# Flamingo block: mLSTM heads weighted in pairs, vector work regrouped around them, the second LoRA weight prepared one stage earlier, one unread matrix product per batch

## The reference, cut to what matters

```python
x = x + tanh(g_xattn[0]) * _L0_xattn_ref(_layernorm(x), ctx, ctx, ...)   # mLSTM
x = x + tanh(g_ffn[0]) * _L0_ffn_ref(_layernorm(x), ...)                 # LoRA FFN
x = x + tanh(g_xattn[1]) * _L1_xattn_ref(_layernorm(x), ctx, ...)        # attention
x = x + tanh(g_ffn[1]) * _L1_ffn_ref(_layernorm(x), ...)                 # mixture of experts
# in the mLSTM, per sequence:
log_f = log_sigmoid(fg); cs = cumsum(log_f)
log_D = where(tril, cs[:, None] - cs[None, :], -inf) + ig
D_mat = exp(log_D - max(log_D))
C = (q @ k.T / sqrt(32)) * D_mat
normalizer = maximum(abs(C.sum(-1)), exp(-max(log_D)))
h = (C / (normalizer + 1e-6)) @ v            # then a layer norm over all heads, times ln_scale
# in the FFN, per weight:
wq = clip(round(w / scale), -128, 127) * scale   # scale = max|w| / 127
h = x @ wq.T + b + 2 * (x @ A.T) @ B.T           # the kernel adds 2 * B @ A to wq once
```

## Time and profile before

| | |
|---|---|
| median of three runs | 1334.13 us |
| the profiled execution | 1336.97 us, span of its instructions 1335.4 us |
| PE busy, over the span | 1203.9 us, 90% |
| DVE, ACT, POOL busy | 872.2, 710.9, 430.8 us |
| mean granted TensorE clock | 0.939 of 2.4 GHz |
| heads stage, first weighing to last update of x | 83.9 to 243.8 us |

### The profile page before, as it was taken

The page is one execution under the profiler, slowest core; times in us unless marked ns, Lnnn a source line. Parts: engine busy times, 40 slices in busy tenths (PEclk is TensorE's granted clock), DMA queues, the critical chain, the costliest instruction groups (busy, mean ns, idle before and its releaser), DMA issues. The chain is left out here.

```text
span 1335.4 us, 28816 instructions
## 1 busy us (share of the span) xinstructions
PE 1203.9 (90%) x9632; PEld 1009.7 (76%) x9633; DVE 872.2 (65%) x2027; ACT 710.9 (53%) x1582; POOL 430.8 (32%) x559
## 2 busy tenths in 40 slices
PE   7868989799999579999999986889989999997998
PEld 3335666698989456666666655879989999997998
DVE  4748778445454457777877755666757677765676
ACT  2357667446354136666666663325655555554553
POOL 1137766523130200111101001476422323221773
PEclk9968888899999869999999997889989999999999
DMA  9144542100000623343433403567745555543773
GB/s 298 54 147 175 179 154 96 48 0 0 0 0 1 113 57 90 82 113 74 97 96 76 97 3 118 204 226 262 228 130 165 172 163 161 179 158 108 269 226 117
DMA packets 97631, 164.71 MB, mean 123 GB/s; under 512 B 12264, under 2 KB 71836, under 8 KB 95228
## 3 DMA queue, kind: packets, MB, share of 16 engines
q1 hardware_dynamic: 87643, 136.11, 33.1%
q0 software_dynamic: 9264, 27.01, 6.4%
q10 hardware_dynamic: 624, 0.32, 0.1%
HBM read 103.66 MB, written 33.69 MB: 103 GB/s over the span
## 5 line engine op out<-in xcount | busy, mean ns | idle before, releaser
L1390 DVE TENSOR_REDUCE c_mx<-c_s 128x2 f32<-128x512 f32 x256 | 164.3, 684 | 74.7 <-PE c_s L1532 74.6
L1313 ACT ACTIVATE c_probs<-c_t 128x512 f32<-128x512 f32 x256 | 139.0, 595 | 8.5 <-PE c_t L1554 5.7
L2346 ACT ACTIVATE de_g_full<-de_hid,d_e_bias 128x256 f32<-128x256 f32 x156 | 77.5, 497 | 105.2 <-PE de_hid L34 105.2
L32 PE MATMUL de_hid<-de_zt_hi,d_e_hi 128*128 128x256 f32 x312 | 90.6, 290 | 1.4 <-DVE de_zt_lo L2370 1.4
L942 ACT ACTIVATE b_g_full<-b_hid,b_b 128x512 f32<-128x512 f32 x64 | 44.3, 692 | 86.8 <-PE b_hid L34 70.4
L1532 PE MATMUL c_s<-c_kt,c_qt 48*128 48x256 f32 x512 | 65.0, 333 | 26.9 <-DVE c_mx L1390 26.9
L34 PE MATMUL de_y_ps<-d_w_hi,de_g_lo 128*128 x312 | 88.2, 283 | 0.0
L32 PE MATMUL de_y_ps<-d_w_hi,de_g_hi 128*128 x312 | 88.1, 282 | 0.0
L33 PE MATMUL de_y_ps<-d_w_lo,de_g_hi 128*128 x312 | 88.0, 282 | 0.0
L1251 POOL CAST c_ct_hi<-c_c_raw 128x512 fp32r<-128x512 f32 x15 | 9.2, 611 | 243.1 <-PE c_misc L34 243.1
L34 PE MATMUL de_hid<-de_zt_hi,d_e_lo 128*128 128x256 f32 x312 | 87.2, 279 | 0.0
(11 more groups left out here) (377 smaller groups left out, 4132.8 us busy)
## 6 DMA issues: line engine op xcount, KB each, us to landing
d_e_raw<-in_w SPq DMA_DIRECT2D x39, 514.0 KB, 3.8
a_mb<-a_maxima SPq DMA_DIRECT2D x16, 1024.0 KB, 4.8
d_z_in<-d_z_rows POOLq DMA_DIRECT2D x39, 256.0 KB, 3.9
d_y_rows<-de_ys SPq DMA_DIRECT2D x39, 256.0 KB, 2.2
c_kt<-c_k_hi SPq DMA_DIRECT2D x64, 128.0 KB, 3.1
c_qt<-c_q_hi SPq DMA_DIRECT2D x64, 128.0 KB, 3.3
d_zt_kept<-d_w_hi SPq DMA_DIRECT2D x32, 256.0 KB, 2.5
d_w_hi<-d_zt_kept SPq DMA_DIRECT2D x16, 512.0 KB, 4.3
```

The source lines that it names most:

```text
L32: tensor.matmul(out, lhs_hi, rhs_hi, start=start, stop=False)
L1313: act.activation(probs[h % PR][:], t_ps[k][:], ACT.Exp).then_inc(exp_done, 1)
L1390: dve.tensor_reduce(mx[n % 2][:, :, k, p:p + 1], s_ps[h % SB][:], AX.X, ALU.max).then_inc(max_done, 1)
L2346: act.activation(g_full[:, m, :], hid[m][:, 0:TOK], ACT.Gelu, bias=bias[u][:, m:m + 1]).then_inc(gelu_full, 1)
```

## The change

Five things are done.

1. `weigh` handles two heads in one instruction (`PAIR = 2`): `a_decay`, `a_c_mat` and `a_qk` become one tensor each, and the instruction reads two banks.
2. On DVE `h_stat` moves behind head 3 and `h_norm` behind head 7. The statistics and the norm for the FFN are taken one tile per batch (batches 6 to 9 and 11 to 14) instead of four at once. The w2 steps leave the stage.
3. The w2 steps move to the end of `mlstm_gates`: quantising and adding on DVE, the high part in two pieces on ACT between `turn(7)` and `gates(7)`, the low part on DVE.
4. `a_mb` gets three buffers, so that its load is issued and POOL's `masks` run one batch earlier. On ACT `keep_outputs` for groups 0 and 1 stands behind `decays` of head 3, group 2 behind head 6 and group 3 behind head 7.
5. PE gets one 128x256 product of the identity with `a_ln_s` per batch (1 to 14) ahead of `scores(n, 1)`. It is written to `a_hp` and read by nobody.

```diff
@@ mlstm_gates, scalar
+            def split_w2(half):
+                act.wait_ge(summed_w2, 1)
...
             for n in range(STEPS):
                 turn(n)
+                if n == STEPS - 1:
+                    split_w2(0)
+                    split_w2(1)
                 gates(n)
@@ mlstm_gates, vector
                 if i == STEPS:
+                    quantise(1)
+                    add_delta_w2()
                     low_part()
+                    low_part_w2()
@@ mlstm_heads
-    W2_AT, HI_AT, LO_AT = 2, 7, 8
-    STATS_AT, RSTD_AT, Z_AT = 9, 10, 11
+    STATS_AT, RSTD_AT, Z_AT = 6, 10, 11
+    MR = 3
+    PAIR = 2
+    FILL = 1
@@ sync
-                after(sync, decay_done, 2 * (n - 1) * H)
-                sync.dma_start(mb[u][:], m_dram[n].partition_broadcast(P)).then_inc(m_loaded[u], 16)
+                after(sync, decay_done, 2 * (n + 1 - MR) * H)
+                sync.dma_start(mb[n % MR][:], m_dram[n].partition_broadcast(P)).then_inc(m_loaded[n % MR], 16)
@@ gpsimd
             values(0)
+            masks(1)
             pool.wait_ge(ready, 1)
             for n in range(B + 2):
                 if n >= 2:
                     h_rstds(n - 2)
+                if n + 2 < B:
+                    masks(n + 2)
                 if n + 1 < B:
-                    masks(n + 1)
                     values(n + 1)
@@ scalar
                     decays(n, h)
-                    if n > 0 and h in (0, 2, 3):
-                        keep_outputs(n - 1, max(h, 1))
-                    if h == H - 1:
-                        keep_outputs(n, 0)
+                    if n > 0 and h == H // 2 - 1:
+                        keep_outputs(n - 1, 0)
+                        keep_outputs(n - 1, 1)
+                    if n > 0 and h == H - 2:
+                        keep_outputs(n - 1, 2)
+                    if n > 0 and h == H - 1:
+                        keep_outputs(n - 1, 3)
@@ vector, weigh
-                dve.wait_ge(qk_done, k + 1)
-                dve.wait_ge(decay_done, 2 * k + 2)
-                after(dve, cv_done, k + 1 - CR)
-                dve.scalar_tensor_tensor(out=c_mat[h % CR][:], in0=qk[h % QUAD][:, 0:W], scalar=SCALE, in1=decay[h % DR][:],
-                                         op0=ALU.mult, op1=ALU.mult).then_inc(c_done, 1)
+                dve.wait_ge(qk_done, k + PAIR)
+                dve.wait_ge(decay_done, 2 * (k + PAIR))
+                after(dve, cv_done, k + PAIR - CR)
+                at, banks = slice(h, h + PAIR), slice(h % QUAD, h % QUAD + PAIR)
+                dve.scalar_tensor_tensor(out=c_mat[:, at, :], in0=qk[:, banks, 0:W], scalar=SCALE, in1=decay[:, at, :],
+                                         op0=ALU.mult, op1=ALU.mult).then_inc(c_done, PAIR)
@@ vector, loop
+            def one_more(n, half):
+                if STATS_AT <= n < STATS_AT + BT:
+                    (ffn_aggregate if half else ffn_stat)(n - STATS_AT)
+                if Z_AT <= n < Z_AT + BT and half:
+                    ffn_norm(n - Z_AT)
+
             for n in range(B):
+                for h in range(0, QUAD, PAIR):
                     weigh(n, h)
+                if n >= 2:
+                    h_stat(n - 2)
+                one_more(n, 0)
+                for h in range(QUAD, H, PAIR):
+                    weigh(n, h)
+                if n >= 2:
+                    h_norm(n - 2)
                 if n >= 1:
                     normalise(n - 1)
+                one_more(n, 1)
@@ tensor, between values(n - 1, 2 and 3) and scores(n, 1)
+                if 1 <= n < B - 1:
+                    pe.wait_ge(const_loaded, 16)
+                    pe.wait_ge(ready, 1)
+                    after(pe, hp_read, n - 1)
+                    for _ in range(FILL):
+                        pe.matmul(hp[:, 0, 0:D], ident[:], ln_s[:], start=True, stop=True)
```

More of the change, by code:

```diff
@@ L345, in split_w1 @@
                 act.activation(lora.w1_hi[:, half, :], w_raw[0][:, cols], ACT.Copy).then_inc(hi_done, 1)
+            def split_w2(half):
+                act.wait_ge(summed_w2, 1)
+                blocks = slice(lora.KF // 2 * half, lora.KF // 2 * (half + 1))
+                cols = slice(D * blocks.start, D * blocks.stop)
+                act.activation(lora.w2_hi[:, blocks, :].rearrange("p a b -> p (a b)"), w_raw[1][:, cols], ACT.Copy).then_inc(hi_w2_done, 1)
             for k in range(2 * PIECES):
@@ L469, in _ @@
             dve.wait_ge(lo_done, 1)
+            dve.wait_ge(lo_w2_done, 1)
             dve.wait_ge(b2_scaled, 1)
@@ L559, in mlstm_heads @@
         kt = [first.kt, sb("kt1", [P, J, S])]
-        mb = [first.mb, sb("mb1", [P, H, S])]
-        mb_late = [sb(f"mb_late{i}", [P, H, P]) for i in range(R)]
+        mb = [first.mb] + [sb(f"mb{i}", [P, H, S]) for i in range(1, MR)]
+        mb_late = [sb(f"mb_late{i}", [P, H, P]) for i in range(MR)]
         va = [sb(f"va{i}", [P, J, H, SLOT]) for i in range(R)]
-        decay = [sb(f"decay{i}", [P, W]) for i in range(DR)]
-        c_mat = [sb(f"c_mat{i}", [P, W]) for i in range(CR)]
+        decay = sb("decay", [P, DR, W])
+        c_mat = sb("c_mat", [P, CR, W])
         ot = [sb(f"ot{i}", [P, GROUPS, S]) for i in range(R)]
@@ L569, in mlstm_heads @@
         hz = sb("hz", [P, J, D])
-        qk = [ctx.enter_context(nc.psum_tensor(f"a_qk{i}", [P, 512], F32)) for i in range(QUAD)]
+        qk = ctx.enter_context(nc.psum_tensor("a_qk", [P, QUAD, 512], F32))
         hp = ctx.enter_context(nc.psum_tensor("a_hp", [P, J, 512], F32))
@@ L576, in mlstm_heads @@
         const_loaded = first.const_loaded
-        m_loaded = [first.m_loaded, sem("m_loaded1")]
+        m_loaded = [first.m_loaded] + [sem(f"m_loaded{i}") for i in range(1, MR)]
         kt_loaded = [first.kt_loaded, sem("kt_loaded1")]
@@ L684, in _ @@
                     decays(n, h)
-                    if n == HI_AT and h % 2 == 1:
-                        split_w2(h // 2)
-                    if n > 0 and h in (0, 2, 3):
-                        keep_outputs(n - 1, max(h, 1))
-                    if h == H - 1:
-                        keep_outputs(n, 0)
-            for g in range(1, GROUPS):
+                    if n > 0 and h == H // 2 - 1:
[5 more added lines that the diff above has]
+                        keep_outputs(n - 1, 3)
+            for g in range(GROUPS):
                 keep_outputs(B - 1, g)
@@ L694, in _ @@
                 act.wait_ge(b_zt_done, c + 1)
-                act.activation(lora.zt_hi[:, c, :], qk[c][:], ACT.Copy).then_inc(b_zt_hi_done, 1)
+                act.activation(lora.zt_hi[:, c, :], qk[:, c, :], ACT.Copy).then_inc(b_zt_hi_done, 1)
         @block.vector
@@ L752, in ffn_stats, with ffn_stat @@
[L752 to L764 removed]
+            def ffn_stat(t):
+                dve.wait_ge(x_done, t + 1)
+                dve.bn_stats(b_stats[:, t, :], x_all[:, t, :]).then_inc(b_stats_done, 1)
@@ L766, in _ @@
             for n in range(B):
-                for h in range(H):
+                for h in range(0, QUAD, PAIR):
                     weigh(n, h)
-                    if n >= 2 and h == 0:
-                        h_stat(n - 2)
-                    if h == 2:
-                        if W2_AT <= n < W2_AT + len(w2_steps):
-                            prepare_w2(n - W2_AT)
-                        if n == LO_AT:
-                            dve.wait_ge(w2_hi_done, 4)
-                            dve.tensor_tensor(lora.w2_lo[:].rearrange("p a b -> p (a b)"), lora.w2_raw[:],
-                                              lora.w2_hi[:].rearrange("p a b -> p (a b)"), ALU.subtract).then_inc(w2_lo_done, 1)
-                        if n == STATS_AT:
-                            ffn_stats()
-                        if n == Z_AT:
-                            ffn_norm()
-                    if n >= 2 and h == QUAD + 1:
-                        h_norm(n - 2)
+                if n >= 2:
+                    h_stat(n - 2)
@@ L820, in values @@
                         if j == 0:
-                            pe.matmul(out[:, 0:S], va[u][:, 0, h, :], c_mat[h % CR][:, 0:S], start=True, stop=True)
+                            pe.matmul(out[:, 0:S], va[u][:, 0, h, :], c_mat[:, h % CR, 0:S], start=True, stop=True)
                         else:
-                            pe.matmul(out[:, P:S], va[u][:, 1, h, :], c_mat[h % CR][:, S:W], start=False, stop=True,
+                            pe.matmul(out[:, P:S], va[u][:, 1, h, :], c_mat[:, h % CR, S:W], start=False, stop=True,
                                       skip_group_check=True).then_inc(cv_done, 1)
```

76 lines of the change are left out of this document (30 added, 46 removed).

## The result

The changed kernel takes 1315.69 us (median of four runs, 1314.02 to 1319.46), the kernel before in the same series 1336.47 (1333.78 to 1341.4): ratio 0.9836, 95% interval 0.9806 to 0.9865. The profiled execution took 1315.06, span 1313.5, clock 0.948. The time lies in the range of the prediction, 5.7 above its value.

The account below looks back on a forecast made before the run. DVE's work plus a 0.80 us wait for PE was taken to bound the heads stage. Gains of 27.3 and 0.9 less 0.15 for gates and 4.4 for clock left 23.7 us, giving 1310 us, range 1299 to 1322.

Parts of the forecast that it names:

- What bounds, and `h_stat` as cover: Heads stage: DVE's work plus 0.80 us idle sets the end; `h_stat`'s 0.89 covers PE's refill, 0.1 to 0.2 left.
- The pair: Weighing on DVE: two heads at once last 0.97 us, 0.89 start to start against 0.94, saving 0.2 a batch.
- The batch: Heads stage: a batch after the change takes 7.2 us on DVE with the remaining wait; PE needs 6.96.
- D: Distance on DVE from first weighing of batch 2 to that of batch 15: 125.66 us before, 98 to 103 forecast.
- the extra pieces: DVE in the heads stage: w2 steps leave; statistics cost 1.8 us and FFN norms 3 over their batches.
- the meeting: Heads stage: `h_norm` and the norms meet POOL's masks and contend; without it the sum would be 3 us lower.
- The clock: PE in the heads stage: falls to half clock cost 4.4 us; rival of falls as often as now, about 1317, chance 0.17.
- three falls: PE in the heads stage: three drops to half clock, each costing 1.5 us beyond PE's slack.
- The gates stage: w2 steps at its end cost 0.15 us, with 1.1 cover on DVE; rival that they don't fit, 1313, chance 0.03.
- POOL: Heads stage: rival that POOL becomes the bound through lock-outs and waits, 7.9 us a batch, time 1319, chance 0.07.
- The last batch: End of the heads stage: the last batch gives 0.9 us more.

Follow-up runs that it names:

- the repeat: The changed kernel run again with nothing altered, on another chip: 1380.97 us, ratio 0.9834 to the kernel before.
- the last four runs: Next batch's masks first, with and without the unread product: 1308.12, 1307.29 us; `h_norm` and L741 as SCALAR_TENSOR_TENSOR in the changed kernel and the latter: 1319.45, 1310.7 us.

## Why the prediction was right

- **What bounds, and `h_stat` as cover: right.** A wait of 0.1 to 0.2 for scores was to stay, none did.
- **The pair: right.** 946 ns against 0.97, 0.865 from start to start against 0.89.
- **The batch: too small.** D less 3.7 for the extra pieces is 97.8, or 7.52 a batch, where I had 7.2. The batches without an extra piece took 7.11 to 7.87, four of the five outside the 7.0 to 7.4 that were given. By parts, from one start to the next (forecast in brackets): pairs 3.46 (3.56), `h_stat` 0.96 (0.89), `h_norm` 1.40 (1.01), `normalise` 1.71 (1.61), wait 0 (0.13). The term that was mis-sized is `h_norm`, with POOL's masks moved to where they meet it more often: 13 x 0.39 = 5 us. `normalise` holds L741, stretched in the same way (0.37 in the mean). The batch of the earlier trace rows that gave the price was not undisturbed itself: the first of its two halves took 0.77 us beside POOL's masks and copy, the second 0.40, and in batches without such a meeting the two cost 0.64. The text named the meeting, put 3 us on it and took it for a thing that stays, not one that the change makes larger. Without the meeting the text put the batch at PE's 6.96. With the masks moved eight batches took 6.94 to 7.22, but there DVE is what is full and L741 is still stretched, so it is in part luck that the numbers are so close.
- **The clock: a term that wasn't paid in this profile.** 4.4 us were set aside for three falls. It was 1.00 all through D. In the repeat at 0.93 the ratio was the same and D 3.2 longer, so where the clock did fall the term was not far off. That the time came out so near is luck: a batch too cheap by 4.2 in all and a clock too dear by 4.4 cancel. Forecast D 98.4 + 4.4 = 102.8, measured 101.5 (and 104.7 on another chip).
- **Extra pieces** 3.7 instead of 4.8, from one start to the next: a statistic with its aggregate 0.40 to 0.58, a norm 0.49.
- **The gates stage: right**, nothing lost where 0.15 was expected, 1.36 left of a cover put at 1.1. **POOL** wasn't the bound, and waited 11.4 us for `h_stat`. **The last batch** gave 0.8 against 0.9.
- **The time.** The FFN starts 25.1 earlier; 23.7 were forecast for the whole. From the forecast's 1310.4 to 1315.7 it is 2.3 for the kernel before itself (1336.5 in the series against 1334.1), 3.2 lost in the untouched layers, 1.1 because the medians differ by 20.8 and the two profiled executions by 21.9, and 1.4 the other way for the earlier start. From the FFN's first product to the end, six profiles on chips of about this speed (before, after and the last four runs) took 1089.4 to 1093.0 us, though they differ only ahead of it, so one profile of each doesn't say whether the 3.2 belong to the change. That stays open.

Shown by experiment: that the order on DVE and w2's move carry the gain, that the third buffer is needed with ACT's new order, that the product does nothing that can be measured, that the masks beside `h_norm` cost 9 us. Only argued: which operands make the meeting. The two that were rewritten fit, but no run moved an operand from SBUF to PSUM. Not run: `h_stat` alone at its old place, and ACT's old order with the rest of the change.

## What to carry to other kernels

When a wait is filled by moving work into it, check what the other vector engine (POOL) does at the new moment: an instruction's quiet duration holds only there. Once the bound engine has no gap, a filler for the clock on another engine is worth a run without it. A buffer and an order that was written with it should be tested together.

## What the hardware showed

- An addition to 16 numbers in SBUF took 0.17 us at best, 0.51 beside a POOL multiplication and 0.99 once beside a mask. A norm of 256 columns went from 0.42 to 1.01 us in the mean by the order on DVE and POOL alone. DVE instructions that read one tensor from PSUM (946 and 160 to 175 ns) and the statistics (410) kept their durations beside the same POOL work.
- The Trainium skill ("SBUF — State Buffer", Who interferes with whom) says that a DVE instruction with two SBUF inputs contends with a GpSimd instruction that reads SBUF, that one with a single SBUF input outside the two-port modes does not, and that the later one blocks for the whole of the other. The runs agree on all three: `h_norm` with two SBUF inputs went from 0.48 us to 1.30 beside a mask, the weighing with one kept its 946 ns, and stretched norms ended 0.14 to 0.28 us behind the mask. `h_norm` as TENSOR_SCALAR has one SBUF tensor and was stretched as well; by the rule it would be in a two-port mode. That fits its shorter rest behind the mask (0.15 us against 0.28 for the other form, the same columns), but no run here shows the mode by itself.
- TensorE was granted its full clock over 95 us with 9.7 of them not busy, without the unread product. The changed kernel was granted 1.00 in one profile and 0.93 in another, on another chip.
